# Attention over 16 batches: the scores of two key tiles issued together in four row groups, in two rounds with another tile's outputs between, and a wider shift on TensorE

## What is computed

```python
q = (queries @ Wq + bq).reshape(N, L, H, D)          # N=16, L=64, H=16, D=16
k = (keys @ Wk + bk).reshape(N, S, H, D)             # S=1601
v = (values @ Wv + bv).reshape(N, S, H, D)
sm = jnp.einsum('nlhd,nshd->nlhs', q, k) / math.sqrt(D)
sm = jax.nn.softmax(sm, axis=1)                      # over the 64 queries
attn = jnp.einsum('nlhs,nshd->nlhd', sm, v)
```

## Time and profile before

| | before |
|---|---|
| median of 3 runs | 1549.56 us (1547.29 to 1550.11) |
| the profiled execution | 1547.42 us |
| its span, first to last instruction | 1545.7 us |
| PE busy | 1385.5 us, 90% of the span |
| DVE, ACT, POOL busy | 1244.9, 1151.2, 1104.1 us |
| maxima on DVE (one for a tile) | 208, the first at 33.13 us, that of the last pair's first tile at 702.71 us |

### The profile page before, as it was taken

The page is one execution under the profiler, slowest core; times in us unless marked ns, Lnnn a source line. Parts: engine busy times, 40 slices in busy tenths (PEclk is TensorE's granted clock), DMA queues, the critical chain, the costliest instruction groups (busy, mean ns, idle before and its releaser), DMA issues. The chain is left out here.

```text
span 1545.7 us, 34902 instructions
## 1 busy us (share of the span) xinstructions
PE 1385.5 (90%) x12768; PEld 1020.4 (66%) x12768; DVE 1244.9 (81%) x1686; ACT 1151.2 (74%) x2975; POOL 1104.1 (71%) x1093
## 2 busy tenths in 40 slices
PE   6999999999999999998877777777777899999995
PEld 5888888888888888876433333333333678888884
DVE  4888888888888888897879999999999644666664
ACT  5877777777777777773789999999999334555552
POOL 2987877778888887863569999999999452444441
PEclk9999999999999999999999999999999999999998
DMA  4224121111111111002755030020000016889884
GB/s 132 58 65 109 43 76 44 44 37 43 38 38 40 41 37 44 16 1 29 211 128 88 3 46 1 6 43 2 1 1 1 1 49 249 298 311 302 313 304 148
DMA packets 106868, 133.01 MB, mean 86 GB/s; under 512 B 43274, under 2 KB 97617, under 8 KB 103256
## 3 DMA queue, kind: packets, MB, share of 16 engines
q1 hardware_dynamic: 96872, 61.61, 16.6%
q0 software_dynamic: 9840, 69.36, 12.7%
HBM read 110.47 MB, written 14.49 MB: 81 GB/s over the span
## 5 line engine op out<-in xcount | busy, mean ns | idle before, releaser
L573 POOL TENSOR_TENSOR half<-prob 128x512 f32<-128x512 f32 (+1 forms) x208 | 263.7, 1268 | 124.7 <-ACT prob L614 122.5
L737 DVE TENSOR_REDUCE mx<-ps_s 128x16 fp32r<-128x1024 f32 (+1 forms) x208 | 254.3, 1223 | 90.9 <-PE ps_s L664 90.6
L608 ACT ACTIVATE prob<-ps_s,mx 128x64 f32<-128x64 f32 (+1 forms) x832 | 195.4, 332 | 148.6 <-issue 129.5
L1407 DVE TENSOR_TENSOR state<-ps_u,state 128x1024 f32<-128x1024 f32 x252 | 297.3, 1220 | 7.0 <-POOL state L1270 3.0
L1365 PE MATMUL ps_y<-state,cz 128*32 128x256 f32 x2048 | 247.3, 384 | 1.8 <-DVE zs L1387 1.0
L664 PE MATMUL ps_s<-qbd,kT 64*128 64x256 f32 (+1 forms) x1664 | 234.8, 401 | 0.2
L1365 PEld LDWEIGHTS ps_y<-state,cz 128*32 128x32 f32 x2048 | 108.9, 110 | 105.6 <-issue 29.1
L1347 PE MATMUL ps_u<-x_rows,b_diag 48*128 48x256 bf16 x1024 | 78.3, 272 | 108.6 <-DVE state L1407 105.3
L664 PEld LDWEIGHTS ps_s<-qbd,kT 64*128 64x128 f32 (+1 forms) x1664 | 139.9, 182 | 45.8 <-issue 21.2
L1286 ACT ACTIVATE ps_a<-A,dt 128x256 f32<-128x256 f32 x378 | 160.2, 465 | 10.3 <-DVE state L1403 10.2
L578 POOL TENSOR_TENSOR quarter<-half 128x256 f32<-128x256 f32 (+1 forms) x208 | 153.4, 738 | 16.3
(11 more groups left out here) (267 smaller groups left out, 3608.5 us busy)
## 6 DMA issues: line engine op xcount, KB each, us to landing
raw<-in_ctxT_dram SPq DMA_DIRECT2D x80, 268.0 KB, 2.8
x_rows<-ssm_x SPq DMA_DIRECT2D x96, 64.0 KB
raw<-in_ctxT_dram SPq DMA_DIRECT2D x16, 261.0 KB, 2.8
b_diag<-blank SPq DMA_DIRECT2D x2, 2048.0 KB, 9.0
slot_rows<-blank SPq DMA_DIRECT2D x1, 3483.0 KB, 16.9
xg<-slot_rows SPq DMA_DIRECT2D x27, 128.0 KB, 5.4
ssm_x<-xp SPq DMA_DIRECT2D x6, 384.0 KB, 4.1
back<-y_slots SPq DMA_DIRECT2D x8, 256.0 KB, 4.4
```

The costliest lines, as they stand in the source:

```text
L573: pool.tensor_tensor(half[0:rows, :, :], prob[0:rows, g % SLOTS, :, 0:L // 2], prob[0:rows, g % SLOTS, :, L // 2:L], ALU.add).then_inc(hal ...
L608: nc.scalar.activation(prob[0:rows, g % SLOTS, h, :], part[:, h, :], ACT.Exp, bias=minus_max[0:rows, g % 2, h:h + 1])
L737: nc.vector.tensor_reduce(mx[0:rows, g % 2, :], part, AX_X, ALU.max, negate=True)\
L1407: nc.vector.tensor_tensor(h, flat(ps_u[k % 2][:, :, :]), h, ALU.add).then_inc(state_ready, 1)
```

## The change

The scores of both tiles of a pair are now issued together. A matmul has 32 rows (2 heads) and 128 columns, and the four row groups of the array are in use: in the first round the even tile takes groups 0 and 2 and the odd tile groups 1 and 3, in the second round the other way about, so that in a round each group writes a bank of its own. The second round waits on `scores_ready` for the end of the first, and half of the turn's outputs stand between the two. The first round waits until both buffers are free. The shift covers all eight heads of the second bank (512 columns), and one exponential of 512 columns takes them; the four singles are gone. DVE takes both maxima, then both subtractions; ACT both shifted exponentials, with the job copies between them, then the two others. Values move behind the second shift, the jobs before the shifts.

```diff
-SHIFTED = slice(8, 12)
-DIRECT = range(12, 16)
+SHIFTED = slice(8, 16)
...
+            def scores(p, turn):
+                pair = (2 * p, 2 * p + 1)
+                if turn:
+                    pe.wait_ge(scores_ready, 2 * p + 1)
+                else:
+                    scores_may_start(p, pair)
                 for c in range(KD):
+                    for g in pair:
+                        n, t, rows = tile(g)
+                        side = (turn + g) % 2
+                        for j in range(P // GR):
+                            r = 2 * j + side
+                            group = slice(HQ * DH * r, HQ * DH * (r + 1))
+                            cols = slice(c * HG * L + side * HQ * L, c * HG * L + (side + 1) * HQ * L)
+                            ins = nc.tensor.matmul(ps_s[g % 2][0:rows, j, cols],
+                                                   kT[n % 2][group, c, t * P:t * P + rows],
+                                                   qbd[n % 2][group, c, HQ * side:HQ * (side + 1), :]
+                                                   .rearrange("p h l -> p (h l)"),
+                                                   start=(c == 0 and turn == 0), stop=True, skip_group_check=True)
                 ins.then_inc(scores_ready, 1)
...
+                if p:
+                    pe.wait_ge(sub_ready, 2 * p)
+                    pe.wait_ge(direct_done, 2 * p)
...
                 for kind, n, j in first:
                     job(m, kind, n, j)
                     m += 1
-                if 1 <= i <= PAIRS:
-                    values(i - 1)
                 if i < PAIRS:
-                    shift(2 * i + 1)
-                if i + 1 < PAIRS:
-                    scores(2 * i + 2)
+                    shift(2 * i)
                 for kind, n, j in second:
                     job(m, kind, n, j)
                     m += 1
-                for g in outputs_of(i):
+                if i < PAIRS:
+                    shift(2 * i + 1)
+                if 1 <= i <= PAIRS:
+                    values(i - 1)
+                early, late = halves(outputs_of(i))
+                if i + 1 < PAIRS:
+                    scores(i + 1, 0)
+                for g in early:
                     outputs(g)
                 if i + 1 < PAIRS:
-                    scores(2 * i + 3)
+                    scores(i + 1, 1)
+                for g in late:
+                    outputs(g)
...
             for i in range(PAIRS + 4):
                 if i < PAIRS:
-                    softmax_part(2 * i)
+                    maximum(2 * i)
+                    maximum(2 * i + 1)
+                    subtract(2 * i)
+                    subtract(2 * i + 1)
                 for n in ends(i):
                     take_output(n)
-                if i < PAIRS:
-                    softmax_part(2 * i + 1)
```

More of the change, by code:

```diff
@@ L598, in split, with exponential_shifted @@
                 raise_chunk(act, nc, a, n, c)
-            def exponential(g):
+            def exponential_shifted(g):
                 n, t, rows = tile(g)
-                act.wait_ge(max_ready, g + 1)
                 act.wait_ge(shifted, g + 1)
@@ L606, in exponential, with exponential_rest @@
                 part = ps_s[g % 2][0:rows, :, :].rearrange("p c (h l) -> p (c h) l", h=HC)
-                for h in DIRECT:
-                    nc.scalar.activation(prob[0:rows, g % SLOTS, h, :], part[:, h, :], ACT.Exp,
-                                         bias=minus_max[0:rows, g % 2, h:h + 1])
                 nc.scalar.activation(prob[0:rows, g % SLOTS, SHIFTED, :], part[:, SHIFTED, :], ACT.Exp)\
                     .then_inc(direct_done, 1)
+            def exponential_rest(g):
+                n, t, rows = tile(g)
                 act.wait_ge(sub_ready, g + 1)
@@ L626, in _ @@
                     put_bias(i - 1)
-                exponential(2 * i)
+                exponential_shifted(2 * i)
+                for kind, n, j in jobs_of(i):
+                    job(m, kind, n, j)
+                    m += 1
+                exponential_shifted(2 * i + 1)
+                exponential_rest(2 * i)
+                exponential_rest(2 * i + 1)
                 for n, c in splits_of(i):
                     split(n, c)
[L630 to L637, removed]
             put_bias(PAIRS - 1)
@@ L650, in job @@
                     query_product(nc, sb, a, ps_k[m % 2], n, j).then_inc(product, 1)
[L652 to L660, removed]
-                for c in range(KD):
[L662 to L667, removed]
-                ins.then_inc(scores_ready, 1)
+            def scores(p, turn):
[4 more added lines that the diff above has]
+                    scores_may_start(p, pair)
+                for c in range(KD):
+                    for g in pair:
+                        n, t, rows = tile(g)
+                        side = (turn + g) % 2
[8 more added lines that the diff above has]
+                                                   start=(c == 0 and turn == 0), stop=True, skip_group_check=True)
+                ins.then_inc(scores_ready, 1)
@@ L670, in shift, with scores_may_start @@
+            def scores_may_start(p, pair):
+                for g in pair:
+                    n, t, rows = tile(g)
+                    if t == 0:
+                        if n:
+                            pe.wait_ge(taken, jobs_until("k", n))
+                        pe.wait_ge(qbd_ready, (n + 1) * KD)
+                if p:
+                    pe.wait_ge(sub_ready, 2 * p)
+                    pe.wait_ge(direct_done, 2 * p)
             def shift(g):
@@ L706, in _ @@
             m = 0
-            scores(0)
-            scores(1)
+            scores(0, 0)
+            scores(0, 1)
             for i in range(PAIRS + 3):
                 first, second = halves(jobs_of(i))
-                if i < PAIRS:
-                    shift(2 * i)
                 for kind, n, j in first:
@@ L724, in _, with heads_of, maximum, subtract @@
                     m += 1
-                for g in outputs_of(i):
+                if i < PAIRS:
[6 more added lines that the diff above has]
+                for g in early:
                     outputs(g)
                 if i + 1 < PAIRS:
-                    scores(2 * i + 3)
+                    scores(i + 1, 1)
+                for g in late:
+                    outputs(g)
         @block.vector
         def _(dve):
[L732 to L737, removed]
+            def heads_of(g):
+                return ps_s[g % 2][0:tile(g)[2], :, :].rearrange("p c (h l) -> p (c h) l", h=HC)
+            def maximum(g):
+                rows = tile(g)[2]
+                dve.wait_ge(scores_ready, 2 * (g // 2) + 2)
+                nc.vector.tensor_reduce(mx[0:rows, g % 2, :], heads_of(g), AX_X, ALU.max, negate=True)\
                     .then_inc(max_ready, 1)
+            def subtract(g):
+                rows = tile(g)[2]
                 dve.wait_ge(max_ready, g + 1)
@@ L741, in softmax_part @@
                     dve.wait_ge(pv_done, g - SLOTS + 1)
-                nc.vector.tensor_tensor(prob[0:rows, g % SLOTS, 0:HC, :], part[:, 0:HC, :],
+                nc.vector.tensor_tensor(prob[0:rows, g % SLOTS, 0:HC, :], heads_of(g)[:, 0:HC, :],
                                         minus_max[0:rows, g % 2, 0:HC].unsqueeze(2).broadcast_to([rows, HC, L]), ALU.add)\
```

## The result

The changed kernel takes 1536.69 us (median of five runs, 1534.46 to 1541.0) against 1549.56; the ratio is 0.9922, 95% interval [0.9903, 0.9941]. It is faster by 12.9 us, where 30 were forecast. The profiled execution took 1538.26 us, its span is 1536.5.

The account below looks back on a forecast made before the run. PE bounded the kernel before; afterwards a closed chain through DVE and PE would. 103 turns of 6.21 instead of 6.50 save 30 us, 1547.4 to 1517.5 profiled, so a median of 1519 us; range 1494 to 1550.

Parts of the forecast that it names:

- A round: Scores on PE: 16 rows, four row groups at once, four steps of 0.111 plus 0.11 and 0.09, 0.64 us.
- The chain: Each turn, through DVE and PE: maxima, second shift, values, first round, outputs, second round end last, 6.21 us.
- 0.02 for PE to see the maxima: Second shift on PE: 0.02 to see DVE's maxima, part of 0.37 us with 0.11 weights and 0.24.
- PE's sum: All of PE's own work in a new turn: 5.98 us against 6.59 before.
- ACT's margin of 0.6: Second shifted exponential: starts T + 2.96, under 0.70 long, before T + 4.24; perhaps 0.1 late, 0.5 us of room left.
- the prediction's rival: Score rounds on PE: weight loads don't hide within a row group, round 0.97, turn 6.87, 1588 us; chance 0.06.
- The gain of 3.07: Skill's gain for four row groups, 512 columns: score rows become 0.58 against 0.55 before the change of shape.
- the sum: Whole attention loop: 103 turns of 6.21 instead of 6.50, 30 us less.
- The fill and drain around the loop stay: Start and end of the loop: unchanged; POOL sums two tiles instead of one, DVE's second pass is gone.
- two row groups alone: Rival on score rounds: only two row groups run at a time, round 1.09, turn 7.11, 1613 us; chance 0.09.
- as cheap as outputs: Rival on score rounds: a round costs 0.56, chain 6.05, PE's sum 5.82, 1503 us; chance 0.15.
- a second chain: Rival: job copies or POOL's sums end last, 0.3 lost each turn, turn 6.5, 1550 us; chance 0.10.

Follow-up runs that it names:

- adjacent: Changed kernel with both rounds of scores following each other and all outputs behind them; 1509.91 us, 0.9741 of the kernel before.
- narrow: Changed kernel with the old shift of 256 columns and four single exponentials ahead of the wide one on ACT; 1604.09 us, 1.0357 of the kernel before.
- early: Changed kernel with the first later batch's splits moved ahead on ACT and POOL; 1534.36 us, 0.9895 of the kernel before.
- fill_early: Changed kernel with filling matmuls in turns without jobs and the first later batch's splits earlier; 1526.77 us, 0.9849 of the kernel before.
- adj_early: Changed kernel with both score rounds side by side and the first later batch's splits earlier, no filling; 1506.36 us, 0.9715 of the kernel before.
- the filled version: Changed kernel with twice six unread matmuls of 256 columns on PE in each turn without jobs; 1532.35 us, 0.9883 of the kernel before.
- before2: The kernel before the change, run once more unaltered, one execution with a profile; 1549.72 us.
- two_groups: Changed kernel with even then odd tile's scores in the old two-row-group form, no wait between rounds; 1606.8 us, 1.037 of the kernel before.

## Why the prediction was right in the turn and wrong in the total

The steps of the turn held. A round is 0.66 against 0.64, with four rows in flight; one tile's outputs 0.57 against 0.56. The chain can be followed in one turn, from the start of the maxima on DVE, with the subtractions, ACT's second shifted exponential and PE's first round:

```profile
326.63 2.36 DVE L752 TENSOR_REDUCE mx<-ps_s 128x16 fp32r<-128x1024 f32 x2 [0.99 <-PE ps_s L662]
328.90 1.28 DVE L761 TENSOR_TENSOR prob<-ps_s,mx 128x512 f32<-128x512 f32 x2
```

```profile
329.65 0.61 ACT L605 ACTIVATE prob<-ps_s 128x512 f32<-128x512 f32 x1
```

```profile
330.87 0.73 PE L662 MATMUL ps_s<-qbd,kT 32*128 32x128 f32 x16
```

The first round starts 4.24 us after the first maximum, as summed, and the turn is 6.26 against 6.21. One term of that sum, 0.02 for PE to see the maxima, is in no row; from their end (328.99) to the first value matmul (329.36) it is the 0.37 that the prediction has with it. At the full clock the turns without jobs are as long as the rest, and the adjacent version is shorter, so it was the chain and not PE's sum (forecast 5.98) that ended last. Subtractions and exponentials are done at 330.18 and 330.26, before the first round; ACT's margin of 0.6 was real but hung on the wide exponential, as the narrow version shows.

The weights hide behind the row ahead in the same row group: with unhidden ones the prediction's rival has a round of 0.97, and it is 0.66. The Trainium skill ("TensorE: Matmul & The Clock Gate", "Part 3: Packing small matmuls") says that a weight load overlaps matmuls in flight only when its row group differs; the rounds here disagree. The gain of 3.07 that the same section states came out close: as an estimate from that page a round is 0.58 before the change of shape, and here it is 0.57 (0.66 less 0.09).

The step that failed is the sum: it took all 103 turns at 6.21, those without jobs too, and held that "The fill and drain around the loop stay". The profiled execution took 1538.3 us where the prediction had 1517.5 for it. Of the 20.8 us between them 14.5 lie in the loop, 5.7 behind it and 0.6 ahead of it (the loop's start varies from 31.8 to 33.7 among the profiles here). In the loop, 654.1 us against 639.6:

- the first six turns take 43.4 instead of 37.3 (six of 6.21), 6.1 us. At the start the jobs need their chunk one turn after it is split, and the change puts the split behind all exponentials of the pair, on ACT and through it on POOL. The prediction followed ACT's order only up to the release of the buffers. The early version takes this wait away. In the second of these turns the clock also fell (at 41.6 us); where it still falls, in fill_early and adj_early, some 2 us of the 6 remain;
- four turns without jobs take 1.5 more each, 6.1 us, by half clock; the filled version takes this away. The prediction said that these turns would wait for the chain, and priced the wait but not what it does to the clock;
- the other 93 turns take 2.3 us more together. Most are 6.26; at a batch boundary a turn of 5.85 and one of 6.45 come out 0.2 shorter by the two, and the 5.85 is 0.4 from the rest, where the prediction had at most 0.25.

Behind the loop, the output projection's 32 rows took 8.79 us instead of 7.14 (the 8.4 and 6.8 of the expectations are the same without the last row's own length), at a granted clock of 0.76 over the stretch:

```profile
700.46 8.79 PE L825 MATMUL op_ps<-wo,oT 128*128 128x256 f32 x32 [1.28 <-PEq L428]
```

```profile
690.00:700.40 10.40, 6.64 (x121) 1.00 0.00 1
700.40:707.60 7.20, 7.14 (x26) 0.76 0.01 2
```

PE was busy 6.64 of the 10.4 us ahead of it. That adds 1.65 us, and the wait for the last sums 0.6. The other 3.4 us behind the loop lie in stages that the change does not touch, and before2 shows that these can differ by 2.5. The four versions whose projection kept the full clock without filling behind the last pair (fill_early, adjacent, adj_early, two_groups) take 846.2 to 847.0 from the last pair's maximum to the end, against 845.5 in before2; with the 0.6 for the sums, at most 0.9 are left unsettled. What decides whether the projection's clock falls stays open.

Of the rivals, the rows exclude three: with 0.66 a round is neither 1.09 (two row groups alone) nor 0.97 (unhidden weights) nor 0.56 (as cheap as outputs). The fourth, a second chain, is excluded by the waits from 70 to 650 us: none of PE's ahead of a round for ACT or DVE is listed, and DVE waits for POOL's sums in nine turns only, where it waits for scores in 90:

```profile
DVE mx L752 <- PE ps_s L662: 75.9, 90, 1.7
DVE z L768 <- POOL quarter L577: 6.5, 9, 2.3
```

None of the rivals named the clock or the start. That 1537 lies within the range up to 1550 is luck: that bound was the price of the second chain, which did not come about.

## What to carry to other kernels

When work moves within an engine's turn, price the turns that are not like the rest (the first, the last, those with a piece missing) by themselves: here the ordinary turn gained 0.37 us, as forecast within 0.05, and ten unusual ones, the first six and four without jobs, lost 12 of the 30 us forecast. A closed chain through two engines is shortened by taking work off it, not by filling a wait that is shorter than the filling: 0.57 us of outputs stood between two rounds that cost only 0.16 more side by side. And where PE begins to wait in every turn, look at the granted clock of each short stretch and not only at its mean, which was still 0.982 here.

## What was not expected of the hardware

A stretch in which PE was busy 1.68 of 3.10 us, in a turn without jobs, was followed by a granted clock of 0.50, though PE was gapless in the turn before. The clock fell in four of ten turns without jobs in one execution of the changed kernel and in three in another; in turn 80 the same stretch was followed by no fall. More matmuls made the turns that were hit shorter (7.7 to 6.26 us).

A change of the array's shape has a price: the first score row starts 0.21 us after the last value matmul (330.66 to 330.87 in the changed kernel), where value matmuls follow each other at 0.12, so it is about 0.09, an estimate from these distances. It is the same on the way to two row groups (324.61 to 324.82 in two_groups). The way back is not separated from the first weights by any row here.
